# A two-layer graph network on one core: own features turned on TensorE from interleaved pairs, GpSimd's element work moved to VectorE, and the order in the gap and the last row changed

## The reference

```
def L0(X, adj, W, b):
    deg = clip(sum(adj, axis=1, keepdims=True) + 1.0, 1.0, None)
    h_neigh = (adj @ X + X) / deg
    out = relu(concatenate([X, h_neigh], axis=1) @ W + b)
    return out / maximum(norm(out, axis=1, keepdims=True), 1e-12)

def L1(x, adj, W):
    for k in range(2):
        x = tanh(concatenate([adj @ x, x], axis=1) @ W[k])
    return x

y = layernorm(x + L0(x, adj, W0, b))
out = layernorm(y + L1(y, adj, W1))
```

## Time and profile before

| | us |
|---|---|
| median of three runs | 1326.22 (1325.09 to 1327.84) |
| profiled execution, its own time | 1325.1 |
| its span in the trace | 1323.3 |
| TensorE matmul busy (PE) | 1200.9 (91%) |
| VectorE busy (DVE) | 1021.0 (77%) |
| ScalarE busy (ACT) | 901.9 (68%) |
| GpSimd busy (POOL) | 154.7 (12%) |

### The profile page before, as it was taken

How to read it: one execution, slowest core, us unless ns; L and a number is a source line. 1 busy time by engine, 2 the same in 40 slices (tenths; PEclk the granted TensorE clock), 3 DMA queues, 4 the chain that set the end, 5 groups by cost and what they waited for, 6 DMA issues and landing times.

```text
span 1323.3 us, 25167 instructions
## 1 busy us (share of the span) xinstructions
PE 1200.9 (91%) x9450; PEld 816.9 (62%) x9450; DVE 1021.0 (77%) x2761; ACT 901.9 (68%) x1309; POOL 154.7 (12%) x118
## 2 busy tenths in 40 slices
PE   3779979989999999989999996999999999989886
PEld 2435646646546556546556555777787878777665
DVE  7888798898887887887787786884655555888996
ACT  5768778778777777777677653765555545877783
POOL 3000020010110110000110003240100000122221
PEclk9999999999999999999999998999999999999998
DMA  9999999999999999999899840000000000000000
GB/s 325 378 382 355 363 367 376 359 359 366 354 354 349 346 349 346 337 337 351 310 341 351 310 158 0 1 1 0 1 1 0 1 0 1 1 8 9 17 17 18
DMA packets 87818, 274.58 MB, mean 207 GB/s; under 512 B 22160, under 2 KB 22160, under 8 KB 87696
## 3 DMA queue, kind: packets, MB, share of 16 engines
q1 hardware_dynamic: 86656, 272.68, 56.1%
q10 hardware_dynamic: 1040, 0.26, 0.1%
HBM read 270.83 MB, written 2.10 MB: 206 GB/s over the span
## 4 chain that ended last, share of the span: by engine, by line
PE 66%; DVE 13%; issue 7%; DMA 6%; POOL 5%; ACT 2%; DVEq 0%; POOLq 0%; ACTq 0%
PE acc L678 29%; PE acc L842 21%; PE ps_pack L669 7%; DMA raw<-in_adj 6%; DVE marks L911 5%; PE ps_epi L707 4%; DVE planes L929 2%; ACT raw L440 2%; PE ps_pack L804 2%; PE ps_pack L802 2%; POOL root L561 1%; DVE packed L916 1%; POOL root L557 1%; PE ps_epi L817 1%; DVE wide L1100 1%
## 5 line engine op out<-in xcount | busy, mean ns | idle before, releaser
L440 ACT ACTIVATE raw<-raw 128x1024 f32<-128x1024 uint32 x512 | 535.7, 1048 | 206.0 <-DVE marks L911 205.0
L678 PE MATMUL acc<-planes,feats 128*128 128x512 fp8e4 x2512 | 567.8, 381 | 7.8 <-issue 7.8
L678 PEld LDWEIGHTS acc<-planes,feats 128*128 128x128 bf16 x2512 | 238.4, 98 | 278.6 <-issue 14.9
L479 ACT ACTIVATE wide<-twos 128x2048 fp32r<-128x2048 fp8e4 x150 | 284.2, 1916 | 160.0 <-PE acc L842 127.1
L911 DVE TENSOR_SCALAR marks<-raw 128x2048 uint8<-128x2048 f32 x256 | 312.6, 1240 | 21.5 <-DMA raw<-in_adj 19.8
L1100 DVE TENSOR_SCALAR wide<-twos 128x2048 fp32r<-128x2048 uint8 x150 | 184.9, 1233 | 78.6 <-PE acc L842 77.7
L669 PE MATMUL ps_pack<-pow,marks 128*128 128x64 bf16 x4096 | 143.3, 194 | 58.0 <-DVE marks L911 57.9
L669 PEld LDWEIGHTS ps_pack<-pow,marks 128*128 128x128 fp8e4 x4096 | 137.2, 99 | 81.4 <-issue 73.9
L1086 DVE TENSOR_SCALAR twos<-packed 128x128 uint32<-128x128 uint32 x600 | 124.6, 270 | 60.8 <-ACT wide L479 53.8
L929 DVE TENSOR_SCALAR planes<-packed 128x128 uint32<-128x128 uint32 x1024 | 150.8, 220 | 23.0 <-DVE packed L916 22.2
L842 PE MATMUL acc<-wide,x_high 128*128 128x512 f32 x512 | 130.0, 400 | 13.3 <-DVE wide L1100 12.9
(11 more groups left out here) (130 smaller groups left out, 872.9 us busy)
## 6 DMA issues: line engine op xcount, KB each, us to landing
raw<-in_adj SPq DMA_DIRECT2D x256, 1024.0 KB, 6.2
out<-result SPq DMA_DIRECT2D x8, 256.0 KB, 2.6
zpart<-in_x SPq DMA_DIRECT2D x7, 256.0 KB, 8.0
zpart<-in_x ACTq DMA_DIRECT2D x1, 256.0 KB, 9.3
w_own<-in_L_gnn_W SPq DMA_DIRECT2D x8, 16.0 KB, 6.5
w_a<-in_L_gnn_W SPq DMA_DIRECT2D x4, 16.0 KB, 6.9
w_y<-in_L_gnn_W SPq DMA_DIRECT2D x2, 16.0 KB, 6.8
w_x<-in_L_gnn_W SPq DMA_DIRECT2D x2, 16.0 KB, 6.9
```

The costliest lines, as they stand in the source:

```text
L440: ins = act.activation(words, words.bitcast(U32), ACT.Sign, accum_out=nonzero[:, tile:tile + 1, I])
L479: act.activation(out_ap, twos[:, u % 2].bitcast(F8), ACT.Abs).then_inc(low_ready, 1)
L678: mm = pe.matmul(acc[g][:, h, :], feats[g][:, I * TB + a, :], planes[:, h, a, :], start=(start or g in opens) and a == 0, stop=a == TB - 1 ...
```

## The change

The two parts of `y_pair` and `x2_pair` stand interleaved now (feature 0 high, feature 0 rest, feature 1 high, ...), and the weights that multiply their sums have each row twice (`w_y_pair`, `w_x2_pair`). The own features of rows k > 0 are no longer added by GpSimd and transposed: TensorE multiplies each part, read at every second element as the stationary operand, by an f32r identity and adds both in PSUM, eight matmuls for four transposes. GpSimd keeps `sum_x1` (into `src`) and the root of the last layernorm, with its scaling; VectorE takes the splits of x2 and the sums and splits of early y. Five turns stand six units behind the row rather than three. From the last stage on (`THIRD`) `two_bits` works for two units at once, in two rooms in turn. The split of y in the first stage is spread over steps 12 and 13, and `keep_y` stands at 14. In the gap, ScalarE, TensorE and VectorE have another order (below). `finish_row` has two instructions fewer on VectorE; the last row is done in halves with a store each.

The diff, cut to its core:

```diff
+THIRD = min(u for u, unit in enumerate(UNITS) if unit[4] and unit[1] <= unit[0])
...
-TURN_AFTER = [3, 7, 11, 17] + [last_of(k) + 3 for k in range(3, 2 * NB - 1)]
+TURN_AFTER = [3, 7, 11, 17] + [last_of(k) + (6 if k < NB else 3) for k in range(3, 2 * NB - 1)]
...
-            for h in range(2):
-                save_acc(NB - 1, h)
...
+            save_acc(NB - 1, 0)
             for u in range(NU + AHEAD + 8):
                 if u < NU:
                     low_bits(u)
+                if u == 1:
+                    save_acc(NB - 1, 1)
...
-            own(1)
-            convert_y(3)
-            split_x2(0)
...
             for k in range(NB, 2 * NB):
                 sum_x1(k)
-                if k == NB:
-                    own(k + 1)
-                if k + 2 < 2 * NB:
-                    own(k + 2)
-                power(k + 11)
+                if k < 2 * NB - 1:
+                    deviation(k + 11)
+            for half in range(2):
+                deviation(2 * NB + 10 + half, slice(TB // 2 * half, TB // 2 * (half + 1)))
...
-                whole = z if k == 0 else src
-                for pair in range(4):
-                    mm = pe.transpose(ps_epi[:, pair * P:(pair + 1) * P], whole[:, pair * P:(pair + 1) * P], ident[:, :])
...
+                    own = y_pair(J) if k < NB else x2_pair(J)
+                    for pair in range(4):
+                        for n in range(2):
+                            mm = pe.matmul(ps_epi[:, pair * P:(pair + 1) * P],
+                                           own[:, 2 * pair:2 * pair + 2, :].rearrange("p t c -> p (t c)")[:, n:4 * D:2], ident_r[:, :],
+                                           start=n == 0, stop=n == 1, skip_group_check=True)
...
+                if pair == 1:
+                    multiply_unit(0)
...
-                        if s == 12:
-                            dve.wait_ge(y_ready, J)
-                            split_three(J - 1, z[:, :], YHI, YLO, NB + J - 1, x1_ready)
-                            if J > 4:
-                                keep_y(J - 1)
+                        if s in (12, 13):
+                            split_y(J - 1, s == 12)
+                        if s == 14 and J > 4:
+                            keep_y(J - 1)
...
+            def two_bits_pair(u):
...
+                for g in range(4):
+                    ins = dve.tensor_scalar(room[:, :, g * NW // 4:(g + 1) * NW // 4], words, 6 - 2 * g, 0xC0C0C0C0,
+                                            ALU.logical_shift_left, ALU.bitwise_and)
+                ins.then_inc(twos_ready, 2)
...
+            expand_unit(3)
             for pair in range(2, 4):
                 drain(NB - 1, 2 * pair, 2, EPI_END - 3 + pair, banks[pair - 2])
...
-                if n in (3, 9):
-                    expand_unit(3 if n == 3 else 4)
+                if n == 3:
+                    expand_unit(4)
...
+                dve.tensor_copy(pair[:, :, 0:2 * D:2], tiles(x2_kept)).then_inc(pair_step, 1)
+                dve.tensor_tensor(pair[:, :, 1:2 * D:2], tiles(z[:, :]), tiles(x2_kept), ALU.subtract).then_inc(x2_ready, 1)
...
             def keep_sum(J):
-                dve.wait_ge(y_summed, 4 - J)
+
+                n = 3 - J
+                dve.tensor_tensor(tiles(y_sum), part(J, YHI), part(J, YMID), ALU.add).then_inc(y_step, 1)
+                dve.wait_ge(y_step, 3 * n + 1)
+                dve.tensor_tensor(tiles(y_sum), tiles(y_sum), part(J, YLO), ALU.add).then_inc(y_step, 1)
...
                 elif n == 2:
-                    ins = dve.tensor_scalar(mean[:, :], mean[:, :], -1.0 / D, None, ALU.mult)
+                    ins = dve.scalar_tensor_tensor(tiles(r), spread(mean[:, :]), -1.0 / D, tiles(r), ALU.mult, ALU.add)
...
-                elif n == 6:
-                    ins = dve.tensor_scalar(stat[:, :], stat[:, :], 1.0 / D, LN_EPS, ALU.mult, ALU.add)
...
+            for n in range(7):
+                for half in range(2):
+                    finish_last(n, half)
```

More of the change, by code:

```diff
@@ L310, in gnn_kernel @@
         normed = sem("normed")
+        last_step = [sem(f"last_step{n}") for n in range(2)]
         out_ready = sem("out_ready")
@@ L584, in add_pair @@
             def add_pair(into, pair, done):
[L585 to L612 removed]
+                pool.tensor_tensor(tiles(into), pair[:, :, 0:2 * D:2], pair[:, :, 1:2 * D:2], ALU.add).then_inc(done, 1)
             def sum_x1(k):
@@ L772, in turn_own @@
             def turn_own(k):
+                read = sum(1 for at in UPPER_AFTER if at is not None and at <= TURN_AFTER[k])
+                if read:
+                    pe.wait_ge(upper_read, read)
                 if k == 0:
@@ L777, in turn_own @@
                     pe.wait_ge(y_ready, NB)
-                else:
-                    pe.wait_ge(own_ready, k)
+                    for pair in range(4):
+                        mm = pe.transpose(ps_epi[:, pair * P:(pair + 1) * P], z[:, pair * P:(pair + 1) * P], ident[:, :])
+                else:
+                    J = ROWS[k]
+                    pe.wait_ge(ident_ready, 1)
                     pe.wait_ge(turn_saved, k)
-                read = sum(1 for at in UPPER_AFTER if at is not None and at <= TURN_AFTER[k])
-                if read:
-                    pe.wait_ge(upper_read, read)
-                whole = z if k == 0 else src
-                for pair in range(4):
-                    mm = pe.transpose(ps_epi[:, pair * P:(pair + 1) * P], whole[:, pair * P:(pair + 1) * P], ident[:, :])
+                    if k < NB:
+                        pe.wait_ge(y_pair_ready, 3 if J >= 4 else 7 - J)
+                    else:
+                        pe.wait_ge(x2_ready, NB - J)
+                    own = y_pair(J) if k < NB else x2_pair(J)
+                    for pair in range(4):
+                        for n in range(2):
+                            mm = pe.matmul(ps_epi[:, pair * P:(pair + 1) * P],
+                                           own[:, 2 * pair:2 * pair + 2, :].rearrange("p t c -> p (t c)")[:, n:4 * D:2], ident_r[:, :],
+                                           start=n == 0, stop=n == 1, skip_group_check=True)
                 mm.then_inc(turned, 1)
             def weigh_own(k):
-                kind, w_of, w, sums = ("one", w_y_self, w_y, agg[1]) if k < NB else ("low", w_x2_self, w_x2, agg[k % 2])
+                kind, w_of, w, sums = ("one", w_y_self, w_y_pair, agg[1]) if k < NB else ("low", w_x2_self, w_x2_pair, agg[k % 2])
                 pe.wait_ge(turn_saved, k + 1)
@@ L844, in multiply_unit @@
                 mm.then_inc(unit_done, 1)
+            for pair in range(4):
+                pe.wait_ge(acc_saved, 2 * NB - 1 + pair // 2)
+                if pair == 1:
+                    pe.wait_ge(pack_saved, ALL)
+                pe.wait_ge(epi_drained, EPI_END - 4 + max(0, pair - 1))
+                weigh(banks[pair % 2], 2 * pair, 2, ONE, 3 * D)
+                if pair == 1:
+                    multiply_unit(0)
             for u in range(NU):
-                multiply_unit(u)
+                if u > 0:
+                    multiply_unit(u)
                 if u == 1:
@@ L1221, in _ @@
+            for u in range(5, NU + 10):
+                if u + 1 < NU:
+                    two_bits(u + 1)
+                for k in range(NB, LAST):
                     if ADD_AFTER[k] + 3 == u:
@@ L1231, in _ @@
                         keep_sum(J)
-                for k in range(2 * NB):
+                for k in range(LAST):
                     if k < NB and ADD_AFTER[k] + 2 == u:
```

205 lines of the change are left out of this document (119 added, 86 removed).

## The result

The changed kernel takes 1275.25 us (1273.58 to 1276.22, four runs) against 1325.65 us of the kernel before (median of four runs): ratio 0.9627, 95% interval 0.9603 to 0.965. A second time it gave 1274.02 us, ratio 0.9613. It is faster, by 50 us where 36 were forecast, inside the range of 1266 to 1310, but outside the forecast's own 1282 to 1298.

What follows compares the result with a forecast made beforehand. No single engine bounds the whole span: TensorE and DMA first, a chain through all engines in the gap, then TensorE, paced last by VectorE. Terms sum to −35.6 us from 1325.1, giving 1290 us after a 1.1 us median offset; range 1266 to 1310.

Steps and rivals of the forecast that it cites:

- Part 1: First stage: splitting y over steps 12 and 13, with keep_y at 14, shortens TensorE's waits for marks; −6 us.
- Part 2: Gap: low_bits first, earlier drains, no GpSimd work beside VectorE's chain, and one expansion out of it; −9 us.
- the sign given: Gap: unit 4 would start at about 818 us less the first stage's gain.
- Part 3: Early units: 10.9 us of work moved to VectorE balances 11 us of stretched two_bits groups; +1 us.
- Part 4: Middle stage: turning three units later removes five waits for zpart and the clock loss behind them; −12.9 us.
- Part 5: The turn: eight f32r matmuls for four transposes cost 0.5 us more each, 7.5 us over 15 turns.
- the rival on the other side: Turns: the strided stationary load is slow; 0.30 us more per load cancels the 36 us gain; chance 0.05.
- Part 6: Last stage: paired masks and a shorter finish_row free VectorE, cutting TensorE's 16.8 us of waits for wide; −8 us.
- Part 7: Tail: the last row in halves hides one half's power under the other's steps; −0.7 us.
- VectorE takes the place: Splits moved from GpSimd hold TensorE: early units pay +9, last stage gains nothing; 1306 us, chance 0.20.
- VectorE wholly released: Last stage: all 16.8 us of waits and 3.7 of clock return, gap gains 3 more; 1278 us, chance 0.14.

Runs made afterwards that it cites:

- e1_split12: Changed kernel with both halves of y's split and keep_y back at step 12: 1288.98 us, ratio 0.9724 against the kernel before.
- e4_gap: Changed kernel with the old order in the gap on ScalarE, TensorE and VectorE: 1283.75 us, ratio 0.97 against the kernel before.
- e5_pool: Changed kernel with the splits of x2 and the sums and splits of early y back on GpSimd: 1279.43 us, ratio 0.967 against the kernel before.
- e2_turn3: Changed kernel with the five middle turns back at three units behind the row: 1292.65 us, ratio 0.9739 against the kernel before.
- e3_single: Changed kernel with two_bits working for one unit at a time in the last stage too: 1286.54 us, ratio 0.9713 against the kernel before.
- e6_finish8: Changed kernel with finish_row's eight steps back on VectorE, save for the last row: 1276.22 us, ratio 0.9638 against the kernel before.
- e7_whole: Changed kernel with the last row finished whole, with one store: 1278.02 us, ratio 0.9662 against the kernel before.

## Why the prediction was right, and where it was short

- *Part 1, first stage: 6 forecast, 13.1 measured; mis-sized.* The cause was as named. By e1_split12 the spread is worth some 11 us behind block 3's turn. From before to after, what lies behind block 1's turn, with all the waits for the split, gained 11.3 us; what lies ahead of it gained 1.9, the loads' chance. The term counted 1.07 us for each of five blocks and almost nothing of the 1.7 us of half clock behind it: 1.2 us of wait (2.60 to 1.41) and 1.7 of clock make 2.9, and the stretches with the waits of blocks 3 and 4 gained 2.8 and 2.4. Over all five blocks the waits fell from 14.6 to 7.2 us, 7.3 rather than 5.4; before, the clock fell behind three of them (1.2 to 1.7 us each), after it behind none. The granted clock during the 24 matmuls that took 7.03 us before (PE busy, PEclk, DMA share, GB/s), and block 5's wait after, 3.70 us before (TensorE's timeline):

```profile
386.00:388.00 2.00, 2.00 (x6) 0.50 0.99 315
569.23 1.09 PE L648 MATMUL ps_pack<-pow,marks 128*128 128x64 bf16 x32 [1.11 <-DVE marks L905]
```

- *Part 2, gap: 9 forecast, 9.4 measured.* By e4_gap 7.2 us is the order (4.8 and 1.4 by the working), by e5_pool 1.9 us GpSimd's work beside the chain (2.9 by the working). Unit 4 starts at 804.66 us, where the sign given was 818 less the first stage's 13.1.
- *Part 3, early units: 1 lost as forecast.* That the number is met is in part luck, since the clock alone moves this stage by 2.8 us. By e5_pool the balance of moved work and stretch holds to 1 to 1.5 us. The longest stretched group before took 3.70 us, not 2.80; the 11 us for all six stand:

```profile
855.54 3.70 DVE L1086 TENSOR_SCALAR twos<-packed 128x128 uint32<-128x128 uint32 x4 [0.66 <-ACT wide L479]
```

- *Part 4, turns: mis-sized.* Their waits and clock were put at 15.4 us; e2_turn3, where a turn's own price is the same on both sides, puts them at 19.3. The waits are 9.9 us as read; the half clock behind three of them costs as much again, since it lasts past the turn. From before to after, without the longer half clock behind the fifth turn, my estimate is 17.8: 11.9 us and four turns' 2.1 in the middle stage, some 3.8 for the fifth (its wait of 2.08 us, and 1.7 of clock).
- *Part 5, the turn: 0.5 us more each forecast, 0.53 measured*, 8 us over 15 turns. A matmul with the strided stationary operand takes 0.11 us, so that the rival on the other side falls. The weight load itself takes 197 ns at every second element and 188 ns for the units' contiguous operand of the same shape (group, us in total, mean ns, idle):

```profile
L826 PEld LDWEIGHTS acc<-wide,x_low 128*128 128x128 f32 x256 | 47.1, 188 | 15.3 <-DVE wide L1129 5.9
L766 PEld LDWEIGHTS ps_epi<-ident_r,x_low 128*128 128x128 f32 x16 | 2.2, 197 | 0.2
```

The rule on SBUF Cachelines of the Trainium skill's page on Advanced Engine Details and Errata, two accesses in each line, agrees with these two rows but for 9 ns.
- *Part 6, last stage: mis-sized.* With the fifth turn's 5.45 us of e2_turn3 taken off, it gained 10.8 us, with the 3.3 that this turn gained by the rows of before and after 12.9; forecast 8. By e3_single the pair alone is worth 14.6 us, by e6_finish8 the shorter `finish_row` 1.7. The waits went nearly as the term had it: 16.8 to 5.5 us, where 5 were left for the bursts of `finish_row`, and less 3.7 for seven turns that makes 7.6. The term took these waits for the most that could come back and left out the clock: 0.98 before, 1.00 after, 0.96 with single units; 0.02 of 186.55 us is some 3.7, of which 1.7 is the fifth turn's. The two make 9.6; some 1 to 3 us of the gain no row here names.
- *Part 7: 0.7 forecast, 1.9 measured,* 1.7 by e7_whole, near the bound of 2.
- *The rivals.* "VectorE takes the place" did not occur: in the last stage it was busy 142.51 of 170.36 us, and the early units lost 0.9 us, not 9. "VectorE wholly released", 1278 us, came nearest in time, but only two thirds of the 16.8 us of waits went; the rest of its 12 us came from the first stage and the turns.

Parts 1, 4 and 6 are short mainly by the same thing: a wait of TensorE was priced at its length, and the half clock behind it at nothing or a part. All three err to one side; that the range still held the time is owed to its lower end, 24 us under the forecast.

In their own stages the undoings lose 16.3, 19.3, 14.6, 7.2, 3.0, 1.7 and 1.7 us, 64 in all; less 8 for the dearer turns that is 56, where the spans differ by 51.6. In e1_split12 and e2_turn3 the clock fell for longer than before the change, so that a part's gain can be read from its undoing only to a few microseconds.

## What to carry to other kernels

A short wait of TensorE can cost twice its length or more, because the clock behind it may be halved for some microseconds (five waits of 1.99 us cost 19.3 us in e2_turn3, one of them 5.45): price a wait by the rows behind it, not by its bracket. Work that is spread over steps has a last place where it can stand, and one step later it costs far more than the spreading gave (some 11 us gained, 41 lost): look for who waits for its result first. Where one engine sets another's pace by a few per cent, two groups of instructions merged into one can bring most of the gain there (14.6 us by e3_single).

## What the runs showed that I had not expected

The same wait does not always cost the same: five turns that waited 1.99 us each in one execution were followed by a halved clock in three cases and by the full clock in two; and the early units of kernels that are alike in them differ by 2.8 us, with a granted clock of 0.95 or 0.98. No run shows which it will be. An f32r matmul of 128 columns with a stationary operand at every second element takes 0.11 us, less than the 0.15 that I had set as its upper bound. And masks of twice the width take 0.89 us rather than 1.26 for two groups: 0.22 against 0.16 us for an instruction, so by an estimate from these two rows about 0.1 us of each is fixed.
